# Swapping the loaded and the streamed operand in the 831 products that count sources of a graph kernel

## The reference

```python
def _L3_gnn_ref(x, W, edge_index):          # the fourth layer
    src = jnp.concatenate([edge_index[0], loops])
    dst = jnp.concatenate([edge_index[1], loops])
    deg = jax.ops.segment_sum(jnp.ones_like(src, dtype=x.dtype), src, num_segments=N)
    deg_rsqrt = jax.lax.rsqrt(deg)
    vals = deg_rsqrt[src] * deg_rsqrt[dst]
    h = x @ W.T
    return jax.ops.segment_sum(vals[:, None] * h[dst], src, num_segments=N)
```

## Time and profile before

| | |
|---|---|
| median of 3 runs | 3418.1 us (3416.4 to 3423.45) |
| the profiled execution's own time | 3423.82 us |
| its span | 3422.0 us |
| busy, share of the span: PE, PE's loads, DVE, ACT, POOL | 92%, 73%, 69%, 46%, 61% |
| pass 2, first to last gather of it | 1446 to 2151 us |
| pass 3, first to last gather of it | 2171 to 2846 us |
| the counting products, first to last | 1481.6 to 2129.0 us |

### The profile page before, as it was taken

The page is one execution under the profiler, slowest core; times in us unless marked ns, Lnnn a source line. Parts: engine busy times, 40 slices in busy tenths (PEclk is TensorE's granted clock), DMA queues, the critical chain, the costliest instruction groups (busy, mean ns, idle before and its releaser), DMA issues.

```text
span 3422.0 us, 57034 instructions
## 1 busy us (share of the span) xinstructions
PE 3143.0 (92%) x18133; PEld 2500.1 (73%) x18133; DVE 2353.6 (69%) x9086; ACT 1589.4 (46%) x3953; POOL 2093.2 (61%) x2041
## 2 busy tenths in 40 slices
PE   6868999999999999899999999899899997999999
PEld 5756676766676776678888887677787775888887
DVE  5657999998999899577777777566676664333333
ACT  3563565655565555444444444344444444232223
POOL 6617777777777777677777777577777772000000
PEclk9988999999999999999999999899999997999999
DMA  6335787777787777766666665766666664444443
GB/s 196 97 141 175 220 251 217 247 229 232 219 249 228 236 238 227 220 192 201 201 198 192 206 199 179 250 199 202 193 204 196 198 183 138 147 148 155 163 163 114
DMA packets 330222, 670.98 MB, mean 196 GB/s; under 512 B 62852, under 2 KB 186336, under 8 KB 329918
## 3 DMA queue, kind: packets, MB, share of 16 engines
q1 hardware_dynamic: 230366, 398.34, 34.6%
q0 software_dynamic: 97616, 267.10, 28.1%
q10 hardware_dynamic: 1936, 1.84, 0.2%
HBM read 489.21 MB, written 177.84 MB: 195 GB/s over the span
## 4 chain that ended last, share of the span: by engine, by line
PE 49%; DMA 20%; DVE 16%; POOL 6%; ACT 4%; issue 4%; POOLq 0%; SPq 0%; ACTq 0%; DVEq 0%
DMA G<-T,idx 18%; PE PS L1826 15%; PE PS L1771 9%; PE PS L1798 7%; POOL G L1884 5%; PE PS L1735 3%; DVE R L1152 3%; PE PS L1800 3%; PE PS L1703 2%; DVE soh L1249 2%; ACT R L1481 2%; PE PS L1724 2%; PE PS L1712 2%; PE PS L1605 2%; PE PS L1606 2%
## 5 line engine op out<-in xcount | busy, mean ns | idle before, releaser
L1884 POOL DMA_INDIRECT G<-T,idx x1926 | 1978.1, 1027 | 711.4 <-issue 304.7
L1771 PE MATMUL PS<-H,aw 128*128 128x256 f32 x3920 | 1016.0, 381 | 0.4 <-DMA aw<-AW 0.4
L1481 ACT ACTIVATE R<-G,wD 128x256 fp32r<-128x256 f32 x1044 | 521.1, 507 | 757.1 <-DMA G<-T,idx 567.8
L1771 PEld LDWEIGHTS PS<-H,aw 128*128 128x128 f32 x3920 | 733.8, 191 | 103.9 <-DMA aw<-AW 0.8
L1152 DVE SCALAR_TENSOR_TENSOR R<-G,wD,R 128x256 fp32r<-128x256 f32 x1044 | 505.6, 484 | 441.9 <-ACT R L1481 437.7
L1798 PE MATMUL PS<-G,M 128*128 128x257 f32 x1764 | 579.0, 412 | 108.2 <-DMA G<-T,idx 51.9
L1800 PE MATMUL PS<-R,Mr 128*128 128x512 f32 x1044 | 601.0, 577 | 51.0 <-DVE R L1152 48.7
L1826 PE MATMUL PS<-HH,cr 128*128 128x512 f32 x2401 | 547.6, 390 | 8.4 <-DVE cr L1318 8.1
L1826 PEld LDWEIGHTS PS<-HH,cr 128*128 128x128 f32 x2401 | 451.1, 188 | 105.3 <-issue 8.5
L1499 ACT CAST atp<-PS 128x512 bf16<-128x512 f32 (+1 forms) x637 | 363.9, 571 | 297.6 <-PE PS L1724 290.4
L1798 PEld LDWEIGHTS PS<-G,M 128*128 128x128 f32 x1764 | 292.8, 198 | 206.9 <-DVE soh L1249 49.6
(11 more groups left out here) (226 smaller groups left out, 3584.4 us busy)
## 6 DMA issues: line engine op xcount, KB each, us to landing
aw<-AW SPq DMA_DIRECT2D x280, 448.0 KB
AT<-atp SPq DMA_DIRECT2D x588, 128.0 KB
br<-AT SPq DMA_DIRECT2D x84, 896.0 KB, 4.8
AW<-awp SPq DMA_DIRECT2D x240, 256.0 KB
G<-T,idx POOLq DMA_INDIRECT x1926
T<-H SPq DMA_DIRECT2D x96, 128.0 KB
X<-in_x SPq DMA_DIRECT2D x8, 768.0 KB, 15.2
T<-tst SPq DMA_DIRECT2D x48, 128.0 KB
```

Of the source, the lines that this page charges most:

```text
L1481: e.activation(R[m % NR][:, 0:D], G[slot][:, 0:D], ACT.Copy, scale=wD[:, k // NC, k % NC:k % NC + 1]).then_inc(s_rw, 1)
L1771: ins = e.matmul(ps, aw[n_ % NAW][:, s_ % 7, :], H[:, s_, :], start=s_ == 0, stop=s_ == NBK - 1)
L1884: e.indirect_dma_start(G[slot][:, 0:D], None, TAB[p][0:N, :], bass.IndirectOffsetOnAxis(ap=idx[:, k // NC, k % NC:k % NC + 1], axis=0)).th ...
```

## The change

The two operands of line 1752 are exchanged: the 49 one-hots of the high digit are loaded, the 128 of the low digit streamed. The counts then come out as 49 partitions of 128 columns. So DVE copies them from PSUM to SBUF at chunk 502 (`degB`, which lies in a buffer that has no further use by then), PE transposes them at chunk 503 into other columns of the same PSUM bank, and DVE adds 1 at chunk 505; the root moves from chunk 503 to 506, the Newton steps from 505 to 508 and the flag from 508 to 511. The one-hots and their layout in `big` stay as they are.

```diff
             out[k].append(("dinv", 0))
             out[k + 3].append(("dinv", 1))
             out[k + 6].append(("dinv", 2))
+            out[k + 9].append(("dinv", 3))
         if engine == 1:
-            out[k + 1].append(("dinv", 0))
+            out[k + 4].append(("dinv", 0))
+        if engine == 2:
+            out[k + 1].append(("dturn",))
...
+        degB = tS[0][0:NBK, 0:P].bitcast(F32)
...
+        s_dgt = sem("s_dgt")
...
                 elif kind == "dinv" and b == 0:
                     w.wait_ge(s_dgs, NDEG)
-                    done(e.tensor_scalar(degS[:, :], PR[:, 0:NBK], 1.0, None, ALU.add), "degS")
+                    done(e.tensor_copy(degB, PR[0:NBK, 0:P]), "degB")
                 elif kind == "dinv" and b == 1:
+                    w.wait_ge(s_dgt, 1)
+                    done(e.tensor_scalar(degS[:, :], PR[:, P:P + NBK], 1.0, None, ALU.add), "degS")
+                elif kind == "dinv" and b == 2:
                     w.wait_ge(s_sq3, 1)
...
+                if kind == "dturn":
+
+                    w.wait_ge(s_v, at["degB"])
+                    e.transpose(PR[:, P:P + NBK], degB, ident[0:NBK, 0:NBK]).then_inc(s_dgt, 1)
                     return
...
-                    ins = e.matmul(PR[:, 0:NBK], column_pair(B, i)[:, :, i % 2], oh[:, :, i], start=c0 + i == 0, stop=c0 + i == EC - 1)
+                    ins = e.matmul(PR[0:NBK, 0:P], oh[:, :, i], column_pair(B, i)[:, :, i % 2], start=c0 + i == 0, stop=c0 + i == EC - 1)
```

More of the change, by code:

```diff
@@ L1691, in behind_ @@
                     return
+                if kind == "dturn":
+                    w.wait_ge(s_v, at["degB"])
+                    e.transpose(PR[:, P:P + NBK], degB, ident[0:NBK, 0:NBK]).then_inc(s_dgt, 1)
+                    return
                 b = BORDER[i]
```

## The result

The changed kernel takes 3450.36 us (median of 4 runs, 3447.13 to 3451.8) against 3417.61 us (median of 4): a ratio of 1.0086, 95% interval 1.0069 to 1.0102, so 0.7 to 1.0% slower. The forecast was no change. Measured again beside the experiments (e15), the ratio was 1.0061, interval 1.0040 to 1.0082.

The account below looks back on a forecast made before the run. POOL's gathers were taken to pace pass 2, hiding PE's 24.5 us saving; with tail and seam costing nothing, the sum was 0 us, so the median stayed at 3418 us, range 3405 to 3429.

Parts of the forecast that it names:

- What bounds the kernel: Pass 2: POOL issues gather after gather with a fixed 0.3 us pause; PE lags without setting the pace.
- PE's need: Pass 2's stretch with counting products: PE's work, summed from start to start, needs 625.5 of 648 us, leaving 22.5 us.
- The counting products: Line 1752, pass 2: 58 ns each instead of 87.5, saving PE 24.5 us, all hidden by POOL's pace.
- the load does not overlap: Rival, line 1752 in pass 2: load and stream add up to 145 ns a product, giving 3443 us; chance 0.09.
- the upper bound of 145 ns: Line 1752: a load as slow as the old stream, 87.5 ns, added without overlap to a 58 ns stream.
- the rival that changes no time: Line 1752: spread-out values cost 1.79 ns each loaded as when streamed, 87.5 ns a product, total 3418 us; chance 0.20.
- The tail: End of pass 2's counts: added DVE copy (0.3 us), PE transpose and later root steps cost nothing; uncovered, about 0.6 us.
- the seam: Passage from pass 2 to pass 3: the last counting product is 29 us earlier, so no effect there.
- The bunches of DVE's work: Pass 2: DVE's work comes in other bunches, shifting the time by over 6.8 us either way; chance 0.09.

Follow-up runs that it names:

- e15: The changed kernel itself, unedited, measured again: 3441.88 us against 3419.44 us for the kernel before, ratio 1.0061.
- e7: The kernel before with every second counting product left out: 3429.25 us against 3422.08 us, ratio 1.0023.
- e10: The changed kernel with high one-hots side by side and 128 columns loaded from each one's start: 3430.32 us against 3422.08 us for the kernel before, ratio 1.0019.
- e16: The kernel before with its own products plus the changed kernel's copy, transpose, waits and later steps: 3420.99 us against 3419.44 us, ratio 0.9999.
- e8: The kernel before with one counting product of each batch made once more: 3423.41 us, ratio 1.0006.
- e9: The kernel before with three counting products of each batch made once more: 3440.9 us against 3422.08 us, ratio 1.0061.
- e6: The kernel before with one product of 64 loaded columns and 1 streamed added to each batch: 3439.03 us against 3413.49 us.
- e1: The changed kernel with 65 columns loaded instead of 49: 3889.79 us against 3886.89 us for the kernel before, both with late gathers.

## Why the prediction was wrong

**What bounds the kernel: right.** POOL paces pass 2 and has no use for a faster PE. e7 takes 37 us of PE away and e10 22 us; neither is faster, and in both the pauses between the gathers are those of the kernel before to 0.2 us.

**PE's need: nearly right; its spare time is smaller than I had it.** My sum left out that the step from the first to the second dense product behind a batch is 257 ns, not 216, and took single rounded distances. With 1.84 us for the way with a batch instead of 1.09 + 0.70 = 1.79 us, the need is 625.5 + 104 x 0.05 = 631 us of 648, and 17 us are to spare, not 22.5. Spare time there is, but 17 us is not a fixed threshold. The length of pass 2 is the gathers' own time and the pauses between them, and the two can be read apart:

| kernel | added to PE, us | pass 2, us | more than 704.4 | gathers' own time, us | pauses more than 161.0 |
|---|---|---|---|---|---|
| before | 0 | 704.4 | 0 | 544.3 | 0 |
| e7, half left out | -37 | 695.0 | -9 | 535.0 | 0 |
| e10, full width | -22 | 709.9 | 5 | 550.1 | 0 |
| e16, tail alone | 0 | 701.7 | -3 | 541.7 | 0 |
| e8, one product more | 9.5 | 697.3 | -7 | 531.3 | 6 |
| e9, three more | 28 | 716.6 | 12 | 534.7 | 22 |
| e6, one narrow | 30.5 | 718.1 | 14 | 535.4 | 23 |
| the change | 34 | 721.3 | 17 | 534.8 | 26 |
| the change again, e15 | 34 | 721.4 | 17 | 533.2 | 28 |

Against the first profile of the kernel before, the lengths behave as if 17 us were free (34 - 17 = 17, 28 - 17 = 11, 30.5 - 17 = 13.5). But the gathers of these kernels took some 9 us less in themselves than there, and where PE sets the pace a shorter gather only waits longer. Measured in pauses, only 4 to 8 us of the added work were free, and e8's 9.5 us already went beyond that. e7's gathers are as short with less work on PE, so PE's lateness is not what shortens them; what sets a gather's own time stays open. The spare time is POOL's pace less PE's need, and POOL's pace alone moved by 9 us between the first profile and e7: it is 4 to 17 us by the gathers that it is measured against.

**The counting products: wrong, and this is the step that failed.** I wrote "All these lines overlap load and stream, so I take 58 ns, or at worst 87.5 ns if the load alone sets the distance". The inner distance came out at the worst case, 91 ns: the load pays for its 16-byte steps as the stream had. But no row that I read had a load of 64 columns or fewer before or behind full ones; line 1628 loads 96. The ends of the batch were never costed. They take 89 + 74 ns more on the way in and 92 + 63 ns more on the way out, 318 of the 325 ns that a batch costs more. e1 (65 columns, none of it) and e6 (one narrow product, nearly all of it) show this. Spread over eight products the new price is 87.5 + 325 / 8 = 128 ns, above the 114.5 ns that I had named as the point from which PE decides and below the upper bound of 145 ns. So the rival "the load does not overlap" gave about the right time, 3443 us, but by another mechanism, so that is luck; the way from PE's excess need to waiting gathers it had right. Its chance of 0.09 was far too low: its only ground for being unlikely was the overlap at full width.

The Trainium skill has a rule that fits, in a page that I had not brought in (TensorEngine Tiling (Array Packing), Key Properties: a change of tiling mode drains TensorE; Tiling Modes lists a 128x64 arrangement). With that rule the runs agree: the cost appears with 49 and 64 columns and not with 65. That an ordinary product with at most 64 loaded columns changes the mode is my inference from this width; no row shows the mode. The skill's rule on cachelines (the Trainium skill, SBUF — State Buffer, Door 1), which I used for the rival that changes no time, held for the load: 1.8 ns a column with steps of 16 bytes, and with the columns side by side 49 loads vanish behind a stream of 57 ns.

**The tail and the seam: right.** The copy took 0.28 us where I took 0.3, and e16 shows no cost; the seam is 19.9 us.

**The bunches of DVE's work: not settled.** e10 has 21 us more of DVE and 22 us less of PE, and its pass 2 is 5 to 15 us longer than in the kernel before, e16 and e7, all of it in the gathers' own time; no run moved DVE's work alone.

## What to carry to other kernels

Before exchanging the loaded and the streamed side of small products, look at the width that is loaded: at 64 columns or fewer among full-width products, count an extra at both ends of every run of them (here 0.3 us in all), and cost a run from the full product before it to the second one behind it. Where two engines look full, add up starts, not durations, and treat the spare time as a threshold that itself moves: of the work added to PE 4 to 17 us were free here, by the gathers' own time, nearly all beyond counted, and work removed brought nothing. Read the pauses of the engine that paces, not only the length of the pass. Read a bound for "an unknown load" as a bound on its surroundings too.

## What the runs showed of the hardware that I had not expected

One product with 64 columns loaded and a single one streamed, between full-width ones, takes 0.29 us of PE's time; with 65 columns, a batch of eight has no such cost. A load of 49 bf16 values 16 bytes apart lasts 187 ns in the records and sets a distance of 91 ns; side by side it lasts 103 ns and is hidden by 128 streamed columns. The first full-width load behind a narrow product starts only when its own product does (2 ns ahead of it, where it was 88 ns ahead behind a full one), and the record of the next product is then 320 ns behind instead of 257, a cost that stands under another line's name. And the same kernel on the same chip took 3841 us at one time and 3419 us at another, the first with gathers that were read 8.4 us after their start instead of 3.9; there the change cost nothing.
